# Multiplying queries by masked key-value blocks first and projecting afterwards: an attention stage reordered, with ScalarE moving results in pieces of 32 partitions

## What is computed

```python
x = x + conv_attention(layer_norm_over_channels(x))
value = depthwise3x3(x, w_v);  query = depthwise3x3(x, w_q).reshape(48, 32, 3136 // 4)
key = depthwise3x3(x, w_k, stride=2).reshape(48, 32, 784 // 4)
v_sampled = bilinear(value, tanh(offset(x) + grid)).reshape(48, 32, 196)
attn = einsum('bcm,bcn->bmn', query, key) * SCALE
out = einsum('bmn,bcn->bcm', attn, v_sampled).reshape(4, 96, 56, 56)
y = einsum('bchw,oc->bohw', out, w_out)
t = tokens(x + y)
t = t + sum over the top 2 of 4 experts of gate * (gelu(ln(t) @ w1 + b1) @ w2 + b2)
```

## Time and profile before

| What | us |
|---|---|
| median of 3 runs (lowest, highest) | 751.4 (750.59, 752.95) |
| span of the profiled execution | 749.4 |
| busy in it: PE, DVE, ACT, POOL | 707.8, 582.8, 384.5, 216.9 |
| attention of batches 0, 1, 2, 3 begins on PE (first kv product) | 98.5 to 579.9 (first and last of 64) |
| first of the last 84 chunks | 637.7 |

### The profile page before, as it was taken

One profiled execution on the slowest core, in us unless ns is written; L12 is line 12 of the kernel. 1 busy time (PEld: TensorE's weight loads), 2 busy tenths in 40 slices (PEclk: granted clock), 3 DMA queues, 4 the chain that ended last, 5 costly groups with the idle time before them and its releaser, 6 DMA issues.

```text
span 749.4 us, 9619 instructions
## 1 busy us (share of the span) xinstructions
PE 707.8 (94%) x3186; PEld 495.8 (66%) x3186; DVE 582.8 (78%) x1511; ACT 384.5 (51%) x722; POOL 216.9 (29%) x184
## 2 busy tenths in 40 slices
PE   5798999799999999999999999999998999999996
PEld 5556566566676666556767566666664665788884
DVE  4889648899999858699999477899975275677774
ACT  2314124744464614744556218545542256899995
POOL 4001700012128610111168201222285121344443
PEclk9998999799999999999999999999999999999999
DMA  8007200044464530345654422435645201121111
GB/s 195 9 0 198 53 9 1 7 98 86 89 185 115 98 56 10 68 103 119 155 129 83 86 48 46 82 80 101 190 102 109 35 20 49 47 69 51 66 47 37
DMA packets 29697, 58.66 MB, mean 78 GB/s; under 512 B 6224, under 2 KB 20176, under 8 KB 29360
## 3 DMA queue, kind: packets, MB, share of 16 engines
q0 software_dynamic: 11584, 17.90, 15.4%
q1 hardware_dynamic: 14336, 32.59, 14.7%
q10 hardware_dynamic: 3728, 7.55, 3.3%
HBM read 30.30 MB, written 14.65 MB: 60 GB/s over the span
## 4 chain that ended last, share of the span: by engine, by line
PE 56%; DVE 19%; DMA 7%; ACT 6%; POOL 5%; issue 5%; POOLq 0%; ACTq 0%
PE py L746 9%; PE pd L662 8%; PE ph L578 7%; DVE val L1133 6%; POOL big L1469 4%; DMA xbuf<-ye 4%; DVE query L1133 3%; PE pa L650 3%; PE pa L529 2%; PE ph L762 2%; PE ph L782 2%; PE ph L784 2%; PE ph L763 2%; PE ph L783 2%; PE ph L764 2%
## 5 line engine op out<-in xcount | busy, mean ns | idle before, releaser
L746 PE MATMUL py<-hid,w 128*96 128x448 f32 x504 | 234.4, 546 | 11.5 <-ACT hid L1006 8.7
L1006 ACT ACTIVATE hid<-ph,b 128x448 f32<-128x448 f32 x252 | 158.9, 632 | 148.1 <-PE ph L764 144.8
L762 PE MATMUL ph<-x_hi,w_hi 96*128 96x448 f32 x252 | 164.4, 653 | 0.0
L1480 POOL DMA_DIRECT2D xbuf<-ye x76 | 66.6, 877 | 327.2 <-DMA xbuf<-ye 163.2
L1469 POOL DMA_INDIRECT big<-value_table,rows x64 | 87.8, 1372 | 90.5 <-DVE rows L1193 56.5
L746 PEld LDWEIGHTS py<-hid,w 128*96 128x96 f32 x504 | 81.6, 165 | 31.2 <-ACT hid L1006 12.6
L763 PE MATMUL ph<-x_lo,w_hi 96*128 96x448 f32 x252 | 93.5, 371 | 0.0
L764 PE MATMUL ph<-x_hi,w_lo 96*128 96x448 f32 x252 | 92.8, 368 | 0.0
L1482 POOL TENSOR_TENSOR xbuf<-xbuf,ye 96x448 f32<-96x448 f32 x36 | 53.9, 1497 | 102.6 <-DVE ye L1416 99.9
L1416 DVE SCALAR_TENSOR_TENSOR ye<-py,b,gate_all 96x448 f32<-96x448 f32 x112 | 75.3, 674 | 9.3 <-PE py L746 7.3
L1443 DVE TENSOR_TENSOR hid_lo<-hid,hid_hi 128x448 fp32r<-128x448 f32 x84 | 59.7, 710 | 27.3 <-ACT hid L1015 27.1
(11 more groups left out here) (165 smaller groups left out, 1081.2 us busy)
## 6 DMA issues: line engine op xcount, KB each, us to landing
gate_all<-gate_rows SPq DMA_DIRECT2D x56, 336.0 KB, 3.5
xbuf<-ye POOLq DMA_DIRECT2D x76, 168.0 KB, 3.4
value_table<-valT ACTq DMA_DIRECT2D x6, 1176.0 KB, 8.9
out<-xbuf SPq DMA_DIRECT2D x28, 168.0 KB, 2.0
xbuf<-in_x SPq DMA_DIRECT2D x3, 1176.0 KB, 10.1
value_table<-valT SPq DMA_DIRECT2D x2, 672.0 KB, 5.3
big<-value_table,rows POOLq DMA_INDIRECT x64, 2.8
value_table<-valT SPq DMA_DIRECT2D x2, 504.0 KB, 5.0
```

The source lines that it names most:

```text
L746: nc.tensor.matmul(py[e % 2][0:C, 0:GPIX], w2[:, c, :], hid[:, k % 3, :], start=(j == 0), stop=(j == CPE - 1)).then_inc(hid_used, 1)
L762: nc.tensor.matmul(bank, w1_hi[:, cols], xh(b, g), start=True, stop=False)
L1006: nc.scalar.activation(hid[:, k % 3, :], ph[k % 2][:, 0:GPIX], ACT.Gelu, bias=b1[:, k % NCH:k % NCH + 1]).then_inc(hid_act, 1)
L1480: pool.dma_start(to, ye[0:C, e, :], accum_op=ALU.add).then_inc(ye_summed, 16)
```

## The change

The order of the products is turned round. kv becomes, for each block i, a 128 x 128 matrix (key rows by value rows, four quarters each; six products of 128 columns a batch), masked by one DVE instruction. `attention` multiplies it by the queries: six full-width products of 392 columns, one for each half h and block i. ACT moves each result to channel order in four pieces of 32 partitions (quarter q, block i), into `val` and `offg`, which is now a tensor of its own; `mix_area` is gone. `attended` multiplies by w_out: one product for a y tile in place of three. The tiles are taken half by half (`Y_TILES`: 0, 2, 4, 6, 1, 3, 5, 7), so that x1 tokens come only from the sixth tile on (`TOKENS_AFTER`). The tables of counts are all new, `SUMS_AHEAD` has one number for all gathers of a batch, and DVE has one more `turn()` after the mask. The core of the diff:

```diff
+HALVES = 2
+Y_TILES = [HALVES * q + h for h in range(HALVES) for q in range(QUARTERS)]
+TOKENS_AFTER = [0, 0, 0, 0, 0, 2, 4, NG]
...
-    order += jobs(1, "xT", NG)[:EARLY_SLOTS] + jobs(0, "keyT", 2) + jobs(1, "xT", NG)[EARLY_SLOTS:] + jobs(0, "mix", QUARTERS) + jobs(0, "x1T", NG) + jobs(1, "pad", 2 * BLOCKS)
+    order += jobs(1, "xT", NG)[:EARLY_SLOTS] + jobs(0, "keyT", 2) + jobs(1, "xT", NG)[EARLY_SLOTS:] + jobs(0, "att", HALVES * BLOCKS) + jobs(0, "x1T", NG) + jobs(1, "pad", 2 * BLOCKS)
...
-        order += jobs(b, "kv", QUARTERS) + jobs(b, "y", NY) + jobs(b, "x1c", NG)
+        order += jobs(b, "kv", 1) + jobs(b, "y", NY) + jobs(b, "x1c", NG)
...
-    dict(valT=(198, 198, 199, 199, 200, 200, 201), keyT=(204, 204), kv=(222, 226, 233, 233), mix=(233, 233, 234, 234),
-         y=(234, 234, 234, 234, 234, 234, 234, 234), x1T=(234, 234, 234, 234, 234, 234, 235),
-         x1c=(241, 241, 243, 243, 249, 249, 250), gateT=(249,)),
...
+    dict(valT=(44, 44, 45, 45, 46, 46, 47), xT=(47, 47, 48, 48, 49, 49, 50), keyT=(50, 51), pad=(69, 69, 70, 70, 70,
+         71), kv=(71,), att=(72, 72, 73, 75, 76, 77), y=(77, 77, 78, 78, 79, 79, 81, 82), x1T=(80, 81, 81, 82, 82, 83,
+         83), offT=(83, 84), x1c=(84, 84, 84, 85, 89, 89, 90), gateT=(89,), offc=(94, 94), offs=(95,)),
...
+    dict(valT=(201, 201, 202, 202, 203, 203, 204), keyT=(207, 207), kv=(230,), att=(231, 231, 233, 234, 235, 236),
+         y=(236, 236, 237, 237, 238, 238, 239, 240), x1T=(239, 239, 239, 240, 240, 241, 241), x1c=(246, 246, 247, 248,
+         252, 252, 252), gateT=(252,)),
...
+    [7, 8, 9, 10, 10, 11, 12, 13, 14, 14, 14, 14, 14, 15, 15, 15, 15, 15, 15, 15, 16, 16, 17, 18, 19, 19, 19, 20, 20,
+     20, 20, 20, 21, 21, 21, 21, 21, 21, 21, 21, 23, 25, 25, 25, 25, 25, 25, 25, 25, 25, 25, 25, 25, 26, 26, 26, 26, 26,
+     26, 26, 26, 26, 26, 26, 26, 26, 27, 27, 27, 27, 27, 27, 27, 27, 27, 27, 27, 27, 27, 27, 28, 28, 28, 28, 28, 28, 28,
+     28, 28, 28, 28, 28, 28, 30, 30, 30, 30, 31, 31, 31, 31, 31, 32],
...
-              (15, 16, 17, 17, 18, 18, 19, 20),
-              (40, 41, 42, 42, 43, 43, 44, 44),
-              (67, 68, 69, 70, 70, 71, 71, 72)]
+              (17, 17, 17, 17, 17, 17, 17, 17),
+              (42, 42, 42, 42, 42, 42, 42, 42),
+              (70, 70, 70, 70, 70, 70, 70, 70)]
...
-        head_mask = sb("head_mask", [C, C])
+        head_mask = sb("head_mask", [128, 128])
...
-        keyT = sb("keyT", [SP, NS, C])
+        keyT = sb("keyT", [SP, 2, BLOCKS, 128])
         kv_area = sb("kv_area", [128, QUARTERS * QUARTERS * C])
-        kv = kv_area[0:C, :].rearrange("d (q i k c) -> d q i k c", q=QUARTERS, i=BLOCKS, k=QUARTERS)
+        kv = kv_area[:, 0:BLOCKS * 128].rearrange("d (i c) -> d i c", i=BLOCKS)
...
-        mix_area = sb("mix_area", [128, QUARTERS * BLOCKS * C])
-        mix = mix_area[:, :].rearrange("c (q i o) -> c q i o", q=QUARTERS, i=BLOCKS)
-        offg = mix_area[0:C, 0:SAMPLES]
+        offg = sb("offg", [C, SAMPLES])
...
+        def att_tile(p0, n):
+
+            if n < NY - 2:
+                i, h = n // HALVES, n % HALVES
+                return val[p0:p0 + CB, i, h * YPIX:(h + 1) * YPIX]
+            return offg[p0:p0 + CB, (n - NY + 2) * YPIX:(n - NY + 3) * YPIX]
+
+        def att_full(n):
+
+            if n < NY - 2:
+                i, h = n // HALVES, n % HALVES
+                return val[0:C, i, h * YPIX:(h + 1) * YPIX]
+            return offg[:, (n - NY + 2) * YPIX:(n - NY + 3) * YPIX]
...
-            def key_values(b, quarters, before=lambda q: None):
-
-                keyq = keyT[:, :, :].rearrange("p (q h) c -> p h q c", h=2)
-                for q in quarters:
-                    before(q)
-                    pe.wait_ge(sampled, b * QUARTERS + q + 1)
-                    bank = dve_bank(b, "kv", q)
+            def key_values(b, before=lambda: None):
+
+                before()
+                pe.wait_ge(sampled, (b + 1) * QUARTERS)
+                bank = dve_bank(b, "kv")
+                values = vs.rearrange("p (q h) c -> p h q c", h=2)
+                for i in range(BLOCKS):
                     for h in range(2):
-                        last = nc.tensor.matmul(bank[0:C, 0:QUARTERS * C], vs[:, 2 * q + h, :], keyq[:, h], start=(h == 0), stop=(h == 1))
-                    last.then_inc(dve_full, 1)
-
-            def mixes(b, before=lambda q: None):
-
-                for q in range(QUARTERS):
-                    before(q)
-                    pe.wait_ge(dve_done, dved(b, "kv", q))
-                    bank = act_bank(b, "mix", q)
-                    for i in range(BLOCKS):
-                        last = nc.tensor.matmul(bank[:, i * C:(i + 1) * C], kv[:, q, i, :, :].rearrange("d k c -> d (k c)"), wout[:, :], start=True, stop=True)
-                    last.then_inc(act_full, 1)
+                        last = nc.tensor.matmul(bank[:, i * 128:(i + 1) * 128], keyT[:, h, i, :], values[:, h, :, i * CB:(i + 1) * CB], start=(h == 0), stop=(h == 1))
+                last.then_inc(dve_full, 1)
+
+            def attention(b, before=lambda n: None):
+
+                for n in range(HALVES * BLOCKS):
+                    before(n)
+                    h, i = n // BLOCKS, n % BLOCKS
+                    if n == 0:
+                        pe.wait_ge(query_conv, b + 1)
+                        pe.wait_ge(dve_done, dved(b, "kv"))
+                    bank = act_bank(b, "att", n)
+                    nc.tensor.matmul(bank[:, 0:YPIX], kv[:, i, :], query[:, i, h * YPIX:(h + 1) * YPIX], start=True, stop=True).then_inc(act_full, 1)
 
             def x1_to_tokens(b, g):
...
-                pe.wait_ge(dve_done, dved(b, "y", g + 1))
+                pe.wait_ge(dve_done, dved(b, "y", QUARTERS + (g + 1) // 2))
...
-                for n in range(NY):
+                tokens = 0
+                for n, tile in enumerate(Y_TILES):
                     before(n)
-                    pe.wait_ge(query_conv, b + 1)
-                    q, h = n // 2, n % 2
-                    pe.wait_ge(act_done, acted(b, "mix", q))
+                    pe.wait_ge(act_done, acted(b, "att", (n // QUARTERS + 1) * BLOCKS - 1))
                     bank = dve_bank(b, "y", n)
-                    for i in range(BLOCKS):
-                        last = nc.tensor.matmul(bank[0:C, 0:YPIX], mix[:, q, i, :], query[:, i, h * YPIX:(h + 1) * YPIX],
-                                                start=(i == 0), stop=(i == BLOCKS - 1))
-                    last.then_inc(dve_full, 1)
-                    if n >= 2:
-                        before_tokens(n - 2)
-                        x1_to_tokens(b, n - 2)
-                before_tokens(NG - 1)
-                x1_to_tokens(b, NG - 1)
+                    nc.tensor.matmul(bank[0:C, 0:YPIX], wout[:, :], att_full(tile), start=True, stop=True).then_inc(dve_full, 1)
+                    while tokens < TOKENS_AFTER[n]:
+                        before_tokens(tokens)
+                        x1_to_tokens(b, tokens)
+                        tokens += 1
...
-            def mixes(b, before=lambda q: None):
-                for q in range(QUARTERS):
-                    before(q)
-                    empty(b, "mix", q, mix[:, q, :, :], 128, BLOCKS * C)
+            def attention(b, before=lambda n: None):
+
+                for n in range(HALVES * BLOCKS):
+                    before(n)
+                    h, i = n // BLOCKS, n % BLOCKS
+                    bank, full = act_job(b, "att", n)
+                    act.wait_ge(act_full, full)
+                    for q in range(QUARTERS):
+                        last = nc.scalar.activation(att_tile(i * CB, HALVES * q + h), pa[bank][q * CB:(q + 1) * CB, 0:YPIX], ACT.Copy)
+                    last.then_inc(act_done, 1)
...
+                turn()
                 if with_head:
                     dve.wait_ge(act_done, acted(b + 1, "pad", 2 * BLOCKS - 1))
 
-                    dve.wait_ge(act_full, acted(b, "mix", QUARTERS - 1))
+                    dve.wait_ge(act_full, acted(b, "att", HALVES * BLOCKS - 1))
...
-                    if m >= 3:
-                        bn(stats_of, b, m - 3, tokens1, "x1T")
+                    for g in tokens_seen(m):
+                        bn(stats_of, b, g, tokens1, "x1T")
                         turn()
...
-                for q in range(QUARTERS):
-                    turn()
-                    dve.wait_ge(dve_full, dved(b, "kv", q))
-                    v.tensor_tensor(kv[:, q, :, :, :].rearrange("d i k c -> d k i c"), pd[dve_job(b, "kv", q)[0]][0:C, 0:QUARTERS * C].rearrange("d (k i c) -> d k i c", k=QUARTERS, i=BLOCKS),
-                                    head_mask[:, :].rearrange("d (o i c) -> d o i c", o=1, i=BLOCKS).to_broadcast([C, QUARTERS, BLOCKS, CB]), ALU.mult).then_inc(dve_done, 1)
+                turn()
+                dve.wait_ge(dve_full, dved(b, "kv"))
+                v.tensor_tensor(kv[:, :, :], pd[dve_job(b, "kv")[0]][:, 0:BLOCKS * 128].rearrange("d (i c) -> d i c", i=BLOCKS),
```

(23 more changed lines are left out.)

51 lines of the change are left out of this document (23 added, 28 removed), and 20 rows, old and new, of the table OUTPUTS_AHEAD.

## The result

The changed kernel takes 777.5 us (773.4 to 781.3, four runs), the kernel before 751.0 us beside it: ratio 1.033, interval 1.030 to 1.037. It is slower by 3.3%; the prediction had 737.3 and 718 to 753. Ratios here compare undisturbed runs alone (two of four for e5, three of four for e8), so one can differ from the ratio of two medians.

What follows compares the result with a forecast made beforehand. PE was taken as the bound with DVE close behind. Batch 0 +2.5, batches 1 and 2 -1.8 each, batch 3 -13 gave -14.1 us on a span of 749.4; forecast 737.3 us, range 718 to 753.

Steps and rivals of the forecast that it cites:

- The likeliest case: Whole kernel: the chain through DVE, ACT and POOL takes over from PE, 728 to 745 us; chance 0.55.
- PE's saving: PE's kv, mix and y products: 101.2 us become 46.4, saving 54.8 us (45.3 to 56.1).
- The pieces: ACT's copies of attended tiles: 24 pieces a batch at 0.46 us each, 11.0 us a batch.
- The rival of dear pieces: ACT's copies between partitions: at 0.67 us a piece they cost 20 us in all, 757 us; chance 0.13.
- The DVE around it: Sampling to statistics of x1, batches 1 and 2: 14.2 us to the first tap plus 21, so 3.2 later each.
- Batch 3: Last batch: 6.5 us earlier at sampling, 1 from the y stage, 5.5 from normalisation, 13 us gained.
- PE's shorter y stage: Batch 3, y products: 1 us gained.
- The gathers: POOL's 16 gathers in one go: sampling ends 3 us earlier in batches 1 and 2, 6.5 in batch 3.
- The normalisation: Stretch after attention: 3 us shorter in batches 1 and 2; 5.5 (2.4 to 8.2) before batch 3's last chunks.
- Batch 0: First batch, without chunks: later first y addition and a late lump of x1T copies lose 2.5 us.
- The waits on sums: POOL's sums, batches 1 to 3: late gathers and masks eat the gain, 751.8 us, no change; chance 0.17.
- my three signs of being wrong: Whole profile: PE full in every stretch, pieces over 0.6 us, or DVE's taps, not its waits, shorter.

Runs made afterwards that it cites:

- e5: The changed kernel's data path with all four tables (chunks, gelus, expert steps, sums) of the kernel before; ratio 1.027, 772 us by it.
- e8: The changed kernel with the four tables of the kernel before and an own buffer for the masked product; 759.7 us, ratio 1.009.
- e2: The changed kernel with two expert steps moved behind the mask and their chunks behind the kv product in batches 1 to 3; 776.9 us, ratio 1.032.
- e4: The changed kernel with one copy per attended tile instead of four pieces, so y comes from other values; 764.8 us, ratio 1.018.
- e6: The changed kernel, its tables kept, with an own buffer for the masked product so taps needn't wait for att products; 777.8 us, ratio 1.035.
- e12: The changed kernel with only a new batch 0 order: next x's statistics and scaling before y additions and x1T copies; 764.0 us, ratio 1.015.
- e13: The kernel before with only batch 0 reordered: next x's statistics and scaling ahead of y additions and x1 copies; 758.2 us, ratio 1.009.
- e1: The changed kernel with the list of sums of the kernel before, sums again between the gathers; 782.5 us, ratio 1.040.
- e3: The changed kernel with sums again among the gathers and no expert step between sampling and the mask; 783.1 us, ratio 1.040.
- e11: The changed kernel with old tables, own masked-product buffer, batch 0 reordered, and the last batch's pieces shared with DVE; 740.7 us, ratio 0.986.
- e9: The changed kernel with old tables, own masked-product buffer, and DVE moving two of four pieces per attended tile in the last batch; 754.3 us, ratio 1.003.

## Why the prediction was wrong

The likeliest case, that the chain through DVE, ACT and POOL takes over from PE, came true in part: PE's share of the chain fell from 56 to 44%, but behind the mask PE is full. The sum was wrong by 36.3 us of span (+22.2 for -14.1): 11.3 in batch 0, 9.0, 8.0 and 7.8 in batches 1 to 3, and 0.2 in the last chunks.

**PE's saving** of 54.8 us was 42.7; as a total it entered no term of the sum. That PE's idle time stays or grows was right.

**The pieces** at 0.46 us measured 0.49. The rival of dear pieces named the side but not the cause: the pieces aren't dear, they are many in a row.

**The DVE around it** is the step that failed in batches 1 and 2. I had 14.2 us to the first off tap and 1 for the expert step ahead of the mask; it was 20.1 and 20.8. The step: I followed the wait on sums on DVE alone and priced it at 1 us. I missed that PE's chunk ahead of kv waits for the same expert steps, so that PE arrives late at kv: the mask came 5.7 and 6.4 us after sampling. From mask to tap I had 12.4 and it took 14.4, with a gelu behind every tile, not three in all, and chunks waiting for them on PE. The tail of 21 us (19 to 24) was right: 20.8. Together 40.8 and 41.5 us instead of 36.2, 4.6 and 5.3 too little. e2 shows that the price of this wait could not simply be had back, and that comes from a term which I put at nothing: "although PE does some ten more chunks in that time". The table has nine more between kv and the last x1T copy in batch 1 (seven in batch 2), 12.2 us at 1.36; they fill PE for 33.81 of the 35.13 us from mask to statistics, where e8 without these nine has 23.42 of 27.67.

**Batch 3.** "- 1 (PE's shorter y stage)" was 8.1 us off: sampling to statistics rose from 32.3 to 39.4. I left out there the 11 us of pieces and the late mask that I had counted in batches 1 and 2. The mask came 5.6 us after sampling (0.5 before) and the first y 15.6 us after the mask (9.8 before); the shorter tail gave 3.7 of these 10.9 us back. Without the pieces (e4) the stage is 37.0 us, so there they are the smaller part.

**The gathers** in one go take 23 to 27 us, near the 22.6 that I took, but start 4 to 11 us later after the offsets' statistics, with two or three more sums ahead. (In batch 2 before, four sums lay between the gathers, not five: the list goes from 40 to 44. No term changes by it.) They gave 0.2, 1.0 and 4.5 us instead of 3, 3 and 6.5: another 6.8 us. DVE's waits for gathers fell in batch 3 to 9.5 us (13.1).

**The normalisation** was right in sum: 1.3, 2.3 and 7.9 us for 3, 3 and 5.5. The last chunks begin at 659.7, not at 623, since all before them is late.

**Batch 0** was 11.3 us off. I added 2.5 us for the first y and the late lump. It lost 4.3 to the first y, 3.9 to the statistics, as x1T's copies wait for additions behind the next x's normalisation on DVE, and 7.0 beyond, of which some 5 are the new tables of batch 0 (37.4 in e6, 32.6 in e8). Of my 2.5, 1.2 were for the first y and 1.3 for the lump; what lies beyond I had at nothing. e12 shows that the changed kernel loses the 3.9 and more by the order, and e13 that the kernel before did not; the clock, which I had not thought of, is a part whose size is open.

**The rivals.** The waits on sums were there, yet e1 and e3 show that giving the sums back doesn't mend it. None of my three signs of being wrong came up: PE was not full in every stretch, the pieces lasted 0.49 us, and the taps kept their length.

The Trainium skill (Perfetto Trace Analysis, Identifying the Most-Contended Engine) has the engine of highest occupancy optimised first, and its warning is that matmul occupancy is not a good measure of how close PE is to roofline. The rows by stretch that I set beside the warning say nothing of roofline. What the runs show is that the ranking by occupancy did not find what to shorten: PE is the busiest engine in the changed kernel and in every experiment on it, 89 to 92%, at 783.1 us (e3) as at 740.7 (e11).

The Trainium skill (TensorEngine Tiling (Array Packing), PSUM Bottleneck) also says that both ScalarE and VectorE should empty PSUM. e9 agrees, with 2.9 us in the one batch where DVE had no taps to make.

Left open: a buffer of its own for the masked product in the kernel before was not tried, so what part of the 1.4% of e11 that would give without the projection is not known; nor is the share of the clock in batch 0, nor which of the four tables costs most.
